# TensorE's loop over taps: the samples between a step's two distances, and 64x64 tiles for the weighted source

## The reference, cut to what matters

```
def deform_conv(x, offset, weight, stride, pad, dil):   # K = 3, pad = dil = 2
    dy = offset[:, 0::2]; dx = offset[:, 1::2]
    ys = base_y + ky * dil + dy;  xs = base_x + kx * dil + dx
    # bilinear: four neighbours of (ys, xs), each times its weight
    sampled = ...
    return einsum('oik,bikhw->bohw', weight, sampled)
off1 = conv2d(x, w_off1, b_off1)
out = relu(bn(deform_conv(x, off1, w_dc1, 1, 2, 2)))
off2 = conv2d(out, w_off2, b_off2)
out = relu(bn(deform_conv(out, off2, w_dc2, 1, 2, 2)) + x)
```

## Time and profile before

| | |
|---|---|
| median of three runs | 966.86 us |
| profiled execution | 967.68 us |
| its span, first to last instruction | 965.7 us |
| mean granted TensorE clock | 0.902 |
| PE / PEld busy | 744.0 us (77%) / 563.6 us (58%) |
| DVE / ACT / POOL busy | 538.7 us (56%) / 452.1 us (47%) / 166.6 us (17%) |
| chain that ended last | PE 65%, ACT 13%, DVE 9%, issue 8% |

### The profile page before, as it was taken

The page is one execution under the profiler, slowest core; times in us unless marked ns, Lnnn a source line. Parts: engine busy times, 40 slices in busy tenths (PEclk is TensorE's granted clock), DMA queues, the critical chain, the costliest instruction groups (busy, mean ns, idle before and its releaser), DMA issues.

```text
span 965.7 us, 39200 instructions
## 1 busy us (share of the span) xinstructions
PE 744.0 (77%) x17378; PEld 563.6 (58%) x17378; DVE 538.7 (56%) x993; ACT 452.1 (47%) x750; POOL 166.6 (17%) x200
## 2 busy tenths in 40 slices
PE   6477777777685676676676676699999999999546
PEld 2255555555423454354354345589999999999434
DVE  2465666656534445445455456346666666666843
ACT  1355556565634544444353453335554444454441
POOL 4000000000000000000000003244444444443210
PEclk8789999999997977888887896789999999999779
DMA  8400000000022000000000006100000000000002
GB/s 208 89 4 1 0 1 0 0 1 0 2 41 37 5 3 5 5 4 5 4 4 4 4 5 157 45 1 2 1 0 0 0 0 0 0 0 0 1 0 89
DMA packets 8146, 17.56 MB, mean 18 GB/s; under 512 B 2149, under 2 KB 6117, under 8 KB 7605
## 3 DMA queue, kind: packets, MB, share of 16 engines
q1 hardware_dynamic: 8022, 15.74, 6.6%
HBM read 11.87 MB, written 3.87 MB: 16 GB/s over the span
## 4 chain that ended last, share of the span: by engine, by line
PE 65%; ACT 13%; DVE 9%; issue 8%; DMA 3%; POOL 1%; SPq 1%; ACTq 0%; DVEq 0%
PE banks L214 13%; PE banks L111 9%; ACT y L238 7%; PE banks L778 7%; PE banks L762 6%; PE banks L808 6%; PE banks L149 5%; PE banks L548 4%; PE banks L819 3%; DVE s L327 3%; PE banks L798 3%; ACT hy L256 2%; PE banks L773 2%; PE banks L195 2%; PE banks L130 2%
## 5 line engine op out<-in xcount | busy, mean ns | idle before, releaser
L214 PE MATMUL banks<-s,y 32*64 32x96 f32 (+2 forms) x9216 | 155.6, 262 | 20.0 <-DVE s L327 16.9
L214 PEld LDWEIGHTS banks<-s,y 32*64 32x64 f32 x9216 | 130.2, 141 | 65.0 <-DVE s L327 39.1
L238 ACT COPY y<-banks 128x768 f32<-128x768 f32 x106 | 84.4, 800 | 153.3 <-PE banks L111 153.3
L327 DVE TENSOR_TENSOR s<-hy,y 128x384 f32<-128x384 f32 x288 | 146.8, 552 | 0.1
L312 DVE TENSOR_SCALAR y<-y 128x384 f32<-128x384 f32 x144 | 51.7, 359 | 150.9 <-ACT y L247 150.8
L149 PE MATMUL banks<-off,near_sel 128*128 (+1 forms) x296 | 63.2, 299 | 75.5 <-ACT y L238 64.8
L247 ACT ACTIVATE y<-banks 128x384 f32<-128x384 f32 x160 | 78.3, 493 | 78.6 <-PE banks L130 77.7
L256 ACT ACTIVATE hy<-banks,row_bias 128x512 f32<-128x512 f32 x148 | 101.6, 686 | 22.1 <-PE banks L149 22.0
L374 POOL COPY stage<-src 128x128 f32<-128x128 f32 x72 | 18.9, 306 | 497.0 <-PE banks L111 497.0
L111 PE MATMUL banks<-w_dc,stage 64*32 64x192 f32 x3392 | 98.5, 343 | 4.5 <-ACT y L238 4.5
L130 PE MATMUL banks<-off,near_sel 128*128 (+2 forms) x640 | 60.7, 225 | 48.5 <-issue 28.4
(11 more groups left out here) (147 smaller groups left out, 1015.7 us busy)
## 6 DMA issues: line engine op xcount, KB each, us to landing
src<-in_x_dram SPq DMA_DIRECT2D x4, 578.0 KB, 5.8
y<-in_w_dram SPq DMA_DIRECT2D x1, 2080.0 KB
off<-in_w_dram SPq DMA_DIRECT2D x2, 1024.0 KB
out_dram<-tokens SPq DMA_DIRECT2D x4, 512.0 KB, 2.6
offsets_dram<-tokens SPq DMA_DIRECT2D x32, 54.0 KB
off<-offsets_dram SPq DMA_DIRECT2D x16, 108.0 KB
near_sel<-in_near_sel_dram SPq DMA_DIRECT2D x1, 960.0 KB
w_dc<-in_w_dc_dram SPq DMA_DIRECT2D x2, 288.0 KB, 10.3
```

What stands on the lines that cost most here:

```text
L214: last = nc.tensor.matmul(out[:, r0:r0 + n, first:first + width], m.yk[32 * j:32 * j + 32, ky, g, col, kx * C:(kx + 1) * C], s_rows(m, cv, ...
L238: nc.scalar.copy(m.yk[:, ky, :, 2 * part:2 * part + 2, :].rearrange("p g a n -> p g (a n)"), slot_banks(m, k)[:, :, 0:384]).then_inc(cv.em ...
L327: nc.vector.tensor_tensor(dst.rearrange("p r g (a c) -> p (r g) a c", a=TC), y, x.rearrange("p r g (a c) -> p (r g) a c", a=TC), ALU.mult) ...
```

## The change

The order in PE's step becomes x distances, samples, y distances, weighted source; in step 0 the zeroing still stands before the samples. The wait for the banks of the y item moves with it, and so do the waits that the weighted source needs. The list of items keeps its order, and ACT's and DVE's programs are not touched. `weighted_near` makes 64 pixels of output at a time, two images of one pair of groups, with 16 matmuls of a 64x64 tile in place of 32 of a 64x32 tile; for that `stage` is laid out with the column of tiles ahead of the pair, POOL's copies write to that layout, and the images change places in `IMAGES`. The distances stay at 128 rows with an address in a register.

```diff
--- before.py
+++ after.py
@@ -34,7 +34,7 @@
 TR, TC = H // TILE_ROWS, W // TILE_COLS
 GUARD = 4
 SLOTS, HY_SLOTS = 3, 3
-IMAGES = [[0, 1, 2, 3], [5, 4, 7, 6]]
+IMAGES = [[0, 2, 1, 3], [5, 7, 4, 6]]
 PARTS = 12
 ROW_COORD, ROW_MOD, ROW_ONE, ROWS_OFF = 12, 13, 19, 20
 OFF_TAIL = 160
@@ -104,14 +104,14 @@
 def weighted_near(nc, m, cv, k, ky, part):
 
     for col in (2 * part, 2 * part + 1):
-        for j in range(4):
+        for half in range(2):
             for g in range(2):
-                image = IMAGES[g][j]
+                image = IMAGES[g][2 * half]
                 rows = slice(C * (image % 2), C * (image % 2) + C)
                 last = nc.tensor.matmul(
-                    m.ps[32 * j:32 * j + 32, FIRST_BANK + 2 * (k % 2) + g, (col % 2) * 192:(col % 2) * 192 + 192],
-                    m.stage[rows, image // 2, col, :], cv.w_dc[rows, 3 * ky:3 * ky + 3, :],
-                    start=True, stop=True, skip_group_check=True)
+                    m.ps[C * half:C * half + C, FIRST_BANK + 2 * (k % 2) + g, (col % 2) * 192:(col % 2) * 192 + 192],
+                    m.stage[rows, col, 2 * g:2 * g + 2, :].rearrange("p a n -> p (a n)"),
+                    cv.w_dc[rows, 3 * ky:3 * ky + 3, :], start=True, stop=True, skip_group_check=True)
     last.then_inc(cv.filled, 1)
 
 
@@ -184,9 +184,6 @@
             pe.wait_ge(cv.emptied, i * PER_ROW + (k - 1))
             columns_near(nc, m, cv, k, tap, new_rows(cv, tap) + TILE_ROWS * later, TILE_ROWS, i)
             k += 1
-            pe.wait_ge(cv.emptied, i * PER_ROW + (k - 1))
-            rows_near(nc, m, cv, k, tap, first_row(cv, tap) + TILE_ROWS * later, i)
-            k += 1
             if t == 0:
                 pe.wait_ge(cv.copied, i + COPIED_FROM)
                 pe.wait_ge(cv.added, i + (ADDED_FROM - 1))
@@ -194,11 +191,6 @@
                 for bank in range(PAIRS):
                     nc.tensor.matmul(m.ps[:, bank, 0:OUT_ROWS * W], m.zeros[:, 0:P], m.zeros[:, 0:OUT_ROWS * W],
                                      start=True, stop=True, skip_group_check=True)
-            if t in STEP_WEIGHTED:
-
-                pe.wait_ge(cv.emptied, i * PER_ROW + (k - 1))
-                if STEP_WEIGHTED[t] == (0, 0, 1):
-                    pe.wait_ge(cv.staged, i * PAIRS + 2 * PAIRS)
             ky, kx = divmod(t, 3)
             n = window(cv)[0]
             r0 = TILE_ROWS + first_row(cv, t)
@@ -216,6 +208,14 @@
                                                 s_rows(m, cv, t)[32 * j:32 * j + 32, :, g, at:at + width],
                                                 start=False, stop=True, skip_group_check=True)
             last.then_inc(cv.sampled, 1)
+            pe.wait_ge(cv.emptied, i * PER_ROW + (k - 1))
+            if t in STEP_WEIGHTED:
+
+                pe.wait_ge(cv.emptied, i * PER_ROW + k)
+                if STEP_WEIGHTED[t] == (0, 0, 1):
+                    pe.wait_ge(cv.staged, i * PAIRS + 2 * PAIRS)
+            rows_near(nc, m, cv, k, tap, first_row(cv, tap) + TILE_ROWS * later, i)
+            k += 1
             if t in STEP_WEIGHTED:
                 weighted_near(nc, m, cv, k, *STEP_WEIGHTED[t][0:2])
                 k += 1
@@ -371,7 +371,7 @@
     for pr in range(PAIRS):
         src = cv.src[:, pr, :].rearrange("p (r c) -> p r c", c=WP)
         rows = src[:, PADR + TILE_ROWS * tile_row:PADR + TILE_ROWS * (tile_row + 1), PADC:PADC + W]
-        nc.gpsimd.tensor_copy(m.stage[:, pr, :, :].rearrange("p a (r c) -> p a r c", c=TILE_COLS),
+        nc.gpsimd.tensor_copy(m.stage[:, :, pr, :].rearrange("p a (r c) -> p a r c", c=TILE_COLS),
                               rows.rearrange("p r (a c) -> p a r c", c=TILE_COLS)).then_inc(cv.staged, 1)
 
 
@@ -1200,7 +1200,7 @@
         m.hx = y_buffer[:, 12288:12288 + 2 * BANK].rearrange("p (s g n) -> p s g n", s=1, g=2)
         m.yk = y_buffer[:, 0:4608].rearrange("p (k g c n) -> p k g c n", k=3, g=2, c=TC)
         m.hx_near = y_buffer[:, 4608:4608 + 2 * TAPS * 384].rearrange("p (s t n) -> p s t n", s=2, t=TAPS)
-        m.stage = sb("stage", [P, PAIRS, TC, TILE_ROWS * TILE_COLS])
+        m.stage = sb("stage", [P, TC, PAIRS, TILE_ROWS * TILE_COLS])
         s_buffer = sb("s", [P, 3072])
         m.s = s_buffer[:, 0:SLOTS * 768].rearrange("p (s n) -> p s n", s=SLOTS)
         m.s_all = s_buffer[:, 0:ALL_SLOTS * 2 * BANK].rearrange("p (s g n) -> p s g n", s=ALL_SLOTS, g=2)
```

## The result

The change makes the kernel slower. The median of four runs is 1055.84 us (1053.1 to 1057.75), and that of the kernel before, measured beside it, is 967.19 us (961.87 to 978.12); the ratio is 1.093, with a 95% interval of 1.088 to 1.099. Forecast were 1050 us and a range of 1002 to 1090. The profiled execution took 1057.75 us, its span is 1055.7 us and its mean granted clock 0.838.

The account below looks back on a forecast made before the run. The prediction saw the kernel bound by two near-equal chains, through the banks and through the distances. 967.7 + 49 - 4 = 1013 us at full clock, plus 40 for slow clock = 1053, called 1050 us, range 1002 to 1090.

Parts of the forecast that it names:

- The wait that goes: Five steps a row, weighted product: the y distances' 0.82 us wait on PE for ScalarE's copy would disappear.
- the one that takes its place: Every step: samples, y distances, Abs, next step's hat, multiplication, next samples form a loop of 3.48 us between samples' starts.
- The row's end: Last samples of a tile row to the next row's first: 4.93 us in the first loop, 6.1 in the second.
- the forecast at full clock: +49 us for the first convolution, -4 us for the second, 1013 us in all with the clock kept.
- The weighted source and S: PE's weighted product with 64x64 tiles stays at 0.81 us, counting zero; sample lengths change by at most 0.07 us, counting zero.
- Code size: Second loop's smaller code covers seven blocks instead of eight, stays loaded, and loses stalls of 5.4 us a row.
- that rival: Second loop's code still fetched every row: 9.5 us row ends, +24 us, slow clock +7, about 1080 us; chance 0.16.
- The clock: Idle PE in steps 1 to 3 lowers the granted clock in part of each row, costing 17 + 23 us; chance 0.50.
- slow interval: Step at half clock, samples to samples: 0.72 us longer; three a row in the first convolution, four in the second.
- full clock (1013 us): Both loops keep full clock with the same 3.48 us interval: 1013 us; chance 0.24.
- The faster one: Multiplication not held by the next step's hats, so the 3.48 us loop doesn't close: near 845 us; chance 0.07.

Follow-up runs that it names:

- mult_first: The changed kernel with VectorE's order turned: x hat of step n+1, multiplication of step n, y hat of step n+1; 885.31 us, ratio 0.908.
- filled: The changed kernel plus four 384-column zero matmuls before the samples in steps 2, 3, 4 and 16 short ones outside the loops; 1025.42 us, ratio 1.054.
- order_alone: The kernel before with only PE's new step order; old 64x32 tiles, images and stage layout; 1078.72 us, ratio 1.106.
- before_shifted: The kernel before with 16 short zero matmuls (32 instructions) ahead of the second convolution, outside the loops; 926.22 us, ratio 0.949.
- before_mult_first: The kernel before with VectorE's order turned alone: x hat of step n+1, multiplication of step n, y hat of step n+1; 966.34 us, ratio 0.994.
- early_copy: mult_first with ScalarE's copy of the finished rows ahead of the y distances' Abs at a row's end; 868.23 us, ratio 0.892.

## Why the prediction was right

**The wait that goes, and the one that takes its place.** Both as said. The forecast put 3.48 us from S to S; the trace has 3.49 to 3.55 in nearly all intervals at full clock behind a row's first, with products and without. Link by link in the step shown: S to Y 0.93 (0.92 forecast), Y to Abs 0.43 (0.42), Abs to hat 0.72 (0.73), hat to multiplication 0.34 (0.34), multiplication to S 1.08 (1.07). mult_first shows that the loop closes through VectorE's order. Where no hats of a next step stand ahead of the multiplication, at the end of each loop, the change itself lets go:

```profile
326.27 1.96 DVE L327 TENSOR_TENSOR s<-hy,y 128x384 f32<-128x384 f32 x4
...
327.34 0.99 PE L206 MATMUL banks<-s,y 32*64 32x80 f32 x64 [0.95 <-DVE s L327]
...
329.82 1.00 PE L206 MATMUL banks<-s,y 32*64 32x64 f32 x64
```

Four multiplications follow each other without a hat, and the last S comes 2.48 us after the one before.

**The row's end.** Forecast 4.93 and 6.1, measured 4.84 and 6.02. The copy of line 297 begins directly behind the Abs, and the addition 2.63 instead of 2.72 us after S.

**What the forecast left out.** The first interval of a row is 3.74 us, not 3.48, through the collision of POOL and VectorE. I had costed POOL's copies at nothing, with the steps beside them as cover; the cover was there, and what I missed was their effect on an instruction on the chain, which in the kernel before ended 0.45 us before they began. Eight times 0.26 us is 2.1 us per convolution. Smaller terms cancel, and so this is the difference between the forecast at full clock and filled: +50.9 against +49, and -1.9 against -4. A further +2.3 us lies between the convolutions. That stretch takes 45.8 us in the kernel before and in order_alone, 46.5 and 47.2 us in before_shifted and before_mult_first, which have the old tiles too, and 46.7 to 48.1 us in the kernels with the new tiles; what does it there stays open.

**The weighted source and S.** Costed at zero, and rightly: W is 0.88 us long in both forms. X follows W's start by 0.94 us, not by 0.81, since it now waits for the Abs of the y distances; that lies inside the idle time and costs nothing. S is 0.99 to 1.00 us.

**Code size.** The forecast said that the second loop would be kept once it covers seven blocks, and no packet of q8 came in its rows behind the first. The Trainium skill's rule in Runtime: NRT & Kernel Launch, Instruction fetch mechanics, that a branch out of the current two pages has to fetch, would give stalls in every row of both loops; none of the kernels has them in the first loop (no packet of q8 in its rows behind the first), and before_shifted loses them in the second by 32 instructions more. Here the measurement decides against it. What I did not see is that the gain has two sizes. I priced it at 5.4 us a row of stalls and, against it, the chain's longer rows, -4 us in sum. In the old order it is worth 48 to 55 us in the second convolution, some 7.5 us a row (34.9 against 27.4 us): about 4.4 of them lie at the row's end (9.5 us against 5.11), about 2 in steps 0 and 2 at the lower clock, the rest in steps 4 and 6, where the shorter stalls of the earlier trace rows are; in the new order 22.6, since the chain's slack hides most of the first stall and the clock is low for another reason. My price for that rival, +24 and +7 us, was 8 us too high: it put both stalls in a line with the chain, while the chain runs on under the first and the second falls behind the first sample.

**The clock.** Forecast 17 + 23 = 40 us, measured 18.1 + 20.9 = 39.0. A slow interval is 4.21 - 3.49 = 0.72 us longer, as worked out. Divided by that, there are 3.1 slow intervals a row in the first convolution and 3.6 in the second (3 and 4 forecast). Their place was off by one: the fall comes around step 2 and lasts into steps 4 and 5, which have a product and in which PE is at work for nearly all of the 4.21 us. So one step of the working failed: the clock did not come back where steps with a product make PE's work nearly solid, but one or two such steps later. The count came out since the fall was as much later as the rise, and that the two errors cancel is luck.

The sum then: 967.68, +50.9 and -1.9 for the chain and the code, +39.0 for the clock, +2.3 between the convolutions, -0.3 elsewhere, 1057.7.

Of the rivals, full clock (1013 us) is what filled shows: 1019.13 profiled, the 6 us being the collision and the stretch between the convolutions. The faster one had its mechanism wrong for this kernel and right for the next: with the loop open, mult_first and early_copy reach 885 and 868, not the 845 that I gave it, because Y's new wait (2.65 us in a step with product) and the row ends (5.0 and 6.2 us in mult_first, 3.9 and 5.1 in early_copy) take the loop's place.

## What to carry to other kernels

Before moving an operation behind another on one engine, follow its result round to the operation that it was moved behind: if the consumer's queue handles the next step's result ahead of this step's, the move closes a loop over all steps, and its length is the sum of all links. Turn the consumer's order round together with the producer's; alone the one gave under 1% here and the other a loss, together they took the kernel with the new tiles from 917.61 to 885.31 us, 3.5%. A gain that consists of removed stalls is worth only what shows beside the longest chain, so two edits are to be costed together and not one by one.

## What was not expected of the hardware

- 32 more instructions ahead of a loop of 1,652 made this program 5% faster (926.22 against 974.89 us), because the second loop's code was no longer fetched again in every row; where it is fetched again, PE stalls at the jump back for 3.8 to 4.3 us (3.2 to 3.9 in order_alone), and in most rows a second time for 0.9 to 1.6 us.
- Matmuls of zeros in idle time of TensorE made it faster by 30 us (1055.84 to 1025.42) by holding the granted clock at 1.00 in nearly all rows. In the change PE idled up to 2.00 us of each interval without a product, and the clock fell in every row; with the zeros it idled 1.35 us, and the clock fell in one row of the fourteen behind each loop's first.
- Four POOL copies of 128x128 numbers go from 1.05 to 1.98 us where they start within 0.2 us of VectorE's multiplications of two SBUF operands, and those from 1.02 to 1.24 us.
